# The last pass of a four-layer graph kernel: one-hot products over 128 columns, and another split between fetching and gathering

## The reference

```python
e = jnp.concatenate((x_i, x_j - x_i), axis=1)      # x_i = x[row], x_j = x[col]
h = jnp.einsum('ec,oc->eo', e, W)                  # 64 outputs
h = h * inv + (bn_beta - bn_mean * inv)            # folded batch norm
h = h * jax.nn.sigmoid(h)
x_out = jax.ops.segment_sum(h, row, num_segments=3125)
```

## Time and profile before

| | |
|---|---|
| median of the runs | 4616.29 us |
| the profiled execution's own time | 4610.87 us |
| its span | 4609.1 us |
| TensorE matmul busy | 3653.8 us (79%) |
| VectorE busy | 2905.1 us (63%) |
| GpSimd busy | 2938.6 us (64%) |
| ScalarE busy | 802.6 us (17%) |
| mean granted clock | 0.868 |

### The profile page before, as it was taken

One profiled execution on the slowest core, in us unless ns is written; L12 is line 12 of the kernel. 1 busy time (PEld: TensorE's weight loads), 2 busy tenths in 40 slices (PEclk: granted clock), 3 DMA queues, 4 the chain that ended last, 5 costly groups with the idle time before them and its releaser, 6 DMA issues. The chain is left out here.

```text
span 4609.1 us, 84700 instructions
## 1 busy us (share of the span) xinstructions
PE 3653.8 (79%) x22275; PEld 2687.5 (58%) x22286; DVE 2905.1 (63%) x10170; ACT 802.6 (17%) x2131; POOL 2938.6 (64%) x2961
## 2 busy tenths in 40 slices
PE   1279248888879999997887858888578785889999
PEld 1279125544543444443666646666466664888999
DVE  7987349999981111115888878888788886223544
ACT  0000002222220000001222213222222221100111
POOL 2677768877778888801777747777477773777200
PEclk9999969999989999998999979999799986555555
DMA  4310023334469999994222232222322222333211
GB/s 145 108 35 10 17 68 89 89 90 91 91 161 358 363 356 356 363 356 169 62 63 62 62 58 63 63 62 62 58 63 62 62 62 50 92 90 88 48 38 35
DMA packets 307333, 532.16 MB, mean 115 GB/s; under 512 B 160747, under 2 KB 206092, under 8 KB 305710
## 3 DMA queue, kind: packets, MB, share of 16 engines
q1 hardware_dynamic: 135291, 377.26, 23.5%
q0 software_dynamic: 89024, 112.37, 12.6%
q10 hardware_dynamic: 82800, 40.01, 3.0%
HBM read 469.36 MB, written 59.59 MB: 115 GB/s over the span
## 5 line engine op out<-in xcount | busy, mean ns | idle before, releaser
L967 POOL DMA_INDIRECT arena<-table,arena x1664 | 1715.9, 1031 | 851.4 <-issue 452.0
L1826 PE MATMUL ps<-arena 128*128 128x96 f32 (+6 forms) x9664 | 1571.3, 340 | 475.7 <-DVE arena L1140 153.5
L1826 PEld LDWEIGHTS ps<-arena 128*128 128x128 f32 (+6 forms) x9664 | 1167.8, 211 | 840.3 <-issue 449.4
L1826 PE MATMUL ps<-arena,nodes 125*64 125x500 f32 (+2 forms) x3144 | 653.0, 537 | 34.6 <-DMA arena<-dense 24.0
L921 POOL DMA_INDIRECT rows_src<-stage,stage_at x400 | 482.8, 1207 | 117.2 <-issue 111.2
L1826 PE MATMUL ps<-nodes,arena 125*128 (+1 forms) x2640 | 508.1, 384 | 60.4 <-DVE arena L1626 37.6
L950 POOL DMA_INDIRECT rows_dst<-stage,arena x400 | 403.0, 1008 | 227.3 <-issue 124.3
L1826 PEld LDWEIGHTS ps<-nodes,arena 125*128 125x128 f32 (+1 forms) x2640 | 495.8, 296 | 70.3 <-issue 48.5
L1393 DVE TENSOR_SCALAR arena<-iota_row_b,arena 128x128 f32<-128x128 bf16 x1664 | 458.6, 297 | 0.0
L1826 PEld LDWEIGHTS ps<-arena,nodes 125*64 125x64 f32 (+1 forms) x3144 | 246.3, 137 | 351.0 <-issue 319.3
L1493 DVE TENSOR_TENSOR nodes<-nodes,ps 125x256 f32 (+1 forms) x70 | 27.5, 393 | 610.2 <-PE ps L2034 610.2
(11 more groups left out here) (335 smaller groups left out, 4155.6 us busy)
## 6 DMA issues: line engine op xcount, KB each, us to landing
arena<-dense SPq DMA_DIRECT2D x240, 750.0 KB, 7.3
nodes<-dense SPq DMA_DIRECT2D x60, 750.0 KB, 8.0
dense<-arena ACTq DMA_DIRECT2D x150, 250.0 KB
nodes<-turn_rows SPq DMA_DIRECT2D x140, 256.0 KB, 3.2
arena<-dense SPq DMA_DIRECT2D x60, 500.0 KB, 7.5
arena<-table,arena POOLq DMA_INDIRECT x1664
arena<-rows_dst SPq DMA_DIRECT2D x208, 96.0 KB
arena<-dense SPq DMA_DIRECT2D x6, 2000.0 KB, 22.0
```

What stands on the lines that cost most here:

```text
L967: nc.gpsimd.indirect_dma_start(rows[:, u, k, 0:width], None, frm, bass.IndirectOffsetOnAxis(ap=p[:, c, j, c_other:c_other + 1].bitcast(I32 ...
L1826: return nc.tensor.matmul(to, lhsT, rhs, start=start, stop=stop, skip_group_check=True)
```

## The change

Each block of the two tables gets 64 columns of zeros behind it (`WIDE = 128`), and the pair steps and the local products stream 128 columns in place of 64; the products of `sum_up3` keep their 96. A bank then holds four tiles (`PG = 4`), and the wait for a free bank is made for each 8 steps; the loop still goes round once for 16 steps, now with two such waits in it. TensorE fetches 120 tiles and 296 are gathered; this makes 720 steps and 45 iterations. `store` has 296 places, so the last 120 tiles are gathered into places that the first 120 leave, each unit behind a wait for the sum that reads its place. The tables of one side move to the arena; the zeros of `msg3` and of the tables are written by GpSimd, and VectorE's memset of `msg3` goes.

```diff
-PT = 104
+PT = 120
-PG, PB, PB0, BURST = 8, 4, 4, 16
+PG, PB, PB0, BURST = 4, 4, 4, 8
+WIDE = 2 * D
+SLOTS = T - PT
...
+        gathered_rows = nodes[0:LO, 3:5, :].rearrange("p i (h d) -> p (i h d)", h=HI).rearrange("p (h d) -> p h d", d=WIDE)
...
-        store = carve([128, T, D])
+        local_rows = carve([LO, HI, WIDE])
+        store = carve([128, SLOTS, D])
...
         def lin3(u):
-            return ps[:, 4 + u % 2, 0:K * D].rearrange("p (k d) -> p k d", k=K)
+            return ps[:, 4 + u % 2, :].rearrange("p (k d) -> p k d", k=K)
+        def place_of(t):
+            return t if t < SLOTS else t - SLOTS
...
-            write_projected(table_sb, t1[:], LAYERS + 1)
+            write_projected(table_sb, gathered_rows[:, :, 0:D], LAYERS + 1)
...
             pool.wait_ge(turn_out, 16 * 2)
+            hold(pool, hs_ready, LAYERS + 2)
+            nc.gpsimd.memset(msg3[:, :, :, D:MW], 0.0)
+            nc.gpsimd.memset(local_rows[:, :, D:WIDE], 0.0)
+            nc.gpsimd.memset(gathered_rows[:, :, D:WIDE], 0.0)
+            pool.drain()
+            pool.sem_inc(cleared, 1)
...
                     t = PT + n * K + k
+                    if t >= SLOTS and t % K == 0:
+                        pool.wait_ge(sums_made, place_of(t) // K + 1)
                     nc.gpsimd.indirect_dma_start(
-                        store[:, t, :], None, table,
+                        store[:, place_of(t), :], None, table,
...
-                nc.vector.tensor_copy(group_of(t1, q), projected(q, D, 2 * D, 2 * D)).then_inc(proj_read, 1)
+                nc.vector.tensor_copy(group_of(gathered_rows, q), projected(q, D, 2 * D, 2 * D)).then_inc(proj_read, 1)
...
-            link(nc.vector.memset(msg3, 0.0))
...
-                nc.vector.tensor_tensor(s3[:, u % PR], store[:, u * K:(u + 1) * K, :], lin3(u), ALU.add).then_inc(sums_made, 1)
+                at_ = place_of(u * K)
+                nc.vector.tensor_tensor(s3[:, u % PR], store[:, at_:at_ + K, :], lin3(u)[:, :, 0:D], ALU.add).then_inc(sums_made, 1)
...
-                nc.scalar.copy(store[:, g * PG:(g + 1) * PG, :].rearrange("p t d -> p (t d)"), ps[:, bank, :]).then_inc(rows_kept, 1)
+                sums = ps[:, bank, :].rearrange("p (t d) -> p t d", d=WIDE)[:, :, 0:D]
+                nc.scalar.copy(store[:, g * PG:(g + 1) * PG, :], sums).then_inc(rows_kept, 1)
                 a.wait_ge(rows_kept, g + 1)
-                nc.scalar.copy(ps[:, bank, :], zeros[:]).then_inc(pair_bank_free, 1)
+                nc.scalar.copy(sums, zeros[:, 0:PG * D].rearrange("p (t d) -> p t d", d=D)).then_inc(pair_bank_free, 1)
...
-            with pe.Fori(0, PS // BURST) as i:
-                need3 = load_values(pe, pair_need[0:1, bass.ds(i, 1)], 1, PT // PG + 1)[0]
-                pe.reg_alu(at_least_one, need3, 1, ALU.max)
-                hold(pe, pair_bank_free, at_least_one)
-                for e in range(BURST // K):
-                    offs = load4(pair_off[0:1, bass.ds(i * BURST + e * K, K)], PB0 * 512, 8 * 512 - D)
-                    blks = load4(pair_blk[0:1, bass.ds(i * BURST + e * K, K)], 0, (HI - 1) * D)
-                    pe.wait_ge(turned_made, i * (BURST // K) + (e + 1))
+            pe.wait_ge(cleared, 1)
+            with pe.Fori(0, PS // (2 * BURST)) as i:
+                for e in range(2 * BURST // K):
+                    if e % (BURST // K) == 0:
+                        b = e * K // BURST
+                        need3 = load_values(pe, pair_need[0:1, bass.ds(i * 2 + b, 1)], 1, PT // PG + 1)[0]
+                        pe.reg_alu(at_least_one, need3, 1, ALU.max)
+                        hold(pe, pair_bank_free, at_least_one)
+                    offs = load4(pair_off[0:1, bass.ds(i * 2 * BURST + e * K, K)], PB0 * 512, 8 * 512 - WIDE)
+                    blks = load4(pair_blk[0:1, bass.ds(i * 2 * BURST + e * K, K)], 0, (HI - 1) * WIDE)
+                    pe.wait_ge(turned_made, i * (2 * BURST // K) + (e + 1))
                     for k in range(K):
-                        ins = mm(flat[:, bass.ds(offs[k], D)], ohT3[0:LO, e % PR, k * 128:(k + 1) * 128],
-                                 gathered_table[:, bass.ds(blks[k], D)], start=False, stop=False)
+                        ins = mm(flat[:, bass.ds(offs[k], WIDE)], ohT3[0:LO, e % PR, k * 128:(k + 1) * 128],
+                                 gathered_table[:, bass.ds(blks[k], WIDE)], start=False, stop=False)
...
                 for k in range(K):
-                    ins = mm(lin3(u)[:, k, :], ohT3[0:LO, (PE_ + u) % PR, k * 128:(k + 1) * 128], local_table[:, bass.ds(offs[k], D)], start=k == 0)
+                    ins = mm(lin3(u)[:, k, :], ohT3[0:LO, (PE_ + u) % PR, k * 128:(k + 1) * 128], local_table[:, bass.ds(offs[k], WIDE)], start=k == 0)
```

More of the change, by code:

```diff
@@ L90 @@
 PH = PC * 128 // 2
-PG, PB, PB0, BURST = 8, 4, 4, 16
+PG, PB, PB0, BURST = 4, 4, 4, 8
+WIDE = 2 * D
+SLOTS = T - PT
 PE_, PU, PR, PK = PS // K, T // K, 4, 6
-assert PT % PG == 0 and PS % BURST == 0 and PH <= TABLE_W and BURST <= (PB - 2) * PG and (PE_ + PU) % 2 == 0
+assert PT % PG == 0 and PS % (2 * BURST) == 0 and 512 == PG * WIDE and PH <= TABLE_W and BURST <= (PB - 2) * PG and (PE_ + PU) % 2 == 0
 AB, AP, MW = 7, 68, 96
@@ L404, in gnn_kernel @@
         msg3 = carve([128, PR, K, MW])
-        store = carve([128, T, D])
-        assert used[0] >= high_to
+        local_rows = carve([LO, HI, WIDE])
+        store = carve([128, SLOTS, D])
+        used[0] = max(used[0], high_to)
         pair_off = carve([1, PS], I32)
@@ L598, in gnn_kernel @@
         sums_made = sem("sums_made")
+        cleared = sem("cleared")
         silu_made = sem("silu_made")
@@ L1269, in _ @@
                 link(nc.vector.tensor_scalar(block_of, ps[0:1, bank, 0:T], -1.0, None, ALU.add))
-                link(nc.vector.tensor_scalar(tab_at[:, side, :], block_of, float(3 * D if side else D), None, ALU.mult))
+                link(nc.vector.tensor_scalar(tab_at[:, side, :], block_of, float(3 * D if side else WIDE), None, ALU.mult))
                 link(nc.vector.tensor_scalar(bank_no, block_of, 1.0 / AB, -(0.5 - 0.5 / AB), ALU.mult, ALU.add))
@@ L1313, in _ @@
                 nc.vector.tensor_scalar(tile_col[:, c:c + 1], ps[:, 4, 2 * c:2 * c + 1], iota_p[:, 0:1], float(128 * c), ALU.add, ALU.add)
-            nc.vector.tensor_scalar(blk_i.rearrange("p (b t) -> p b t", b=2), ps[0:1, 2:4, 0:PH], float(D), None, ALU.mult)
+            nc.vector.tensor_scalar(blk_i.rearrange("p (b t) -> p b t", b=2), ps[0:1, 2:4, 0:PH], float(WIDE), None, ALU.mult)
             link(nc.vector.tensor_scalar(step_code[:], ps[:, 4, 0:2 * PC].rearrange("p (c x) -> p x c", x=2)[:, 1, :], 128.0, None, ALU.mult))
@@ L1330, in _ @@
             link(nc.vector.scalar_tensor_tensor(tile_tmp, tile_tmp, -float(PB * PG), tile_row, ALU.mult, ALU.add))
-            link(nc.vector.tensor_scalar(off_i, tile_tmp, float(D), float(PB0 * 512), ALU.mult, ALU.add))
+            link(nc.vector.tensor_scalar(off_i, tile_tmp, float(WIDE), float(PB0 * 512), ALU.mult, ALU.add))
             floor_of(need_f, tile_row[:, BURST - 1:PS:BURST], PG)
@@ L1610, in _ @@
                 v.wait_ge(proj_done, groups_before(LAYERS + 1) + (q + 2))
-                nc.vector.tensor_tensor(group_of(t2, q), projected(q, 0, D, 2 * D), over_group(bnr[:, 1, :], q), ALU.add)
-                nc.vector.tensor_copy(group_of(t1, q), projected(q, D, 2 * D, 2 * D)).then_inc(proj_read, 1)
+                nc.vector.tensor_tensor(group_of(local_rows, q), projected(q, 0, D, 2 * D), over_group(bnr[:, 1, :], q), ALU.add)
+                nc.vector.tensor_copy(group_of(gathered_rows, q), projected(q, D, 2 * D, 2 * D)).then_inc(proj_read, 1)
             v.wait_ge(proj_read, groups_before(LAYERS + 2) + 1)
@@ L1814, in _ @@
                 bank = PB0 + g % PB
-                nc.scalar.copy(store[:, g * PG:(g + 1) * PG, :].rearrange("p t d -> p (t d)"), ps[:, bank, :]).then_inc(rows_kept, 1)
+                sums = ps[:, bank, :].rearrange("p (t d) -> p t d", d=WIDE)[:, :, 0:D]
+                nc.scalar.copy(store[:, g * PG:(g + 1) * PG, :], sums).then_inc(rows_kept, 1)
                 a.wait_ge(rows_kept, g + 1)
-                nc.scalar.copy(ps[:, bank, :], zeros[:]).then_inc(pair_bank_free, 1)
+                nc.scalar.copy(sums, zeros[:, 0:PG * D].rearrange("p (t d) -> p t d", d=D)).then_inc(pair_bank_free, 1)
+            a.wait_ge(cleared, 1)
             for u in range(PU):
@@ L2155, in _ @@
             ins.then_inc(pair_bank_free, PB)
-            gathered_table = nodes[0:LO, 3, :]
-            local_table = nodes[0:LO, 4, :]
-            with pe.Fori(0, PS // BURST) as i:
-                need3 = load_values(pe, pair_need[0:1, bass.ds(i, 1)], 1, PT // PG + 1)[0]
-                pe.reg_alu(at_least_one, need3, 1, ALU.max)
-                hold(pe, pair_bank_free, at_least_one)
-                for e in range(BURST // K):
-                    offs = load4(pair_off[0:1, bass.ds(i * BURST + e * K, K)], PB0 * 512, 8 * 512 - D)
```

(12 more changed lines are left out.)

## The result

| | before | after |
|---|---|---|
| median of 4 runs | 4614.14 us (4607.81 to 4619.28) | 4783.81 us (4777.17 to 4786.21) |
| span of the profiled execution | 4609.1 us | 4784.4 us |
| mean granted clock | 0.868 | 0.876 |

The ratio is 1.0366, with a 95% interval of 1.0348 to 1.0384. The forecast was 4542 us, so the time lies 242 us above it and outside the range.

A forecast was written before the change was run, and what follows sets the result against it. TensorE's line was taken as the bound in the last pass: its sequencer in the first stage, the low clock in the second. +40 - 115 + 1 = -74 us gave a 4542 us median, range 4505 to 4600.

The forecast's parts named there:

- An iteration becomes 7.94 + 0.7 = 8.65 us: Last pass, pair-step loop (first stage): the added bank wait lengthens each of 45 iterations; stage +40 us.
- the comb: First stage, TensorE: 7.10 us of matmuls per iteration, next piece 7.94 us after the one before; forecast 8.6 to 8.7.
- The second bank wait: First stage, TensorE's sequencer: another wait for a free bank per iteration costs 0.7 us, range 0.6 to 0.9.
- The first stage gains nothing from a high clock: Last pass, pair steps: TensorE's sequencer is the bound, so a faster clock is worth nothing there.
- The second stage gets 2.4 GHz from its products of 128 columns: Last pass, local products and sums: a unit takes 2.3 us in place of 3.41, 104 units, -115 us.
- The first rival: Second stage: clock stays at 1.2 GHz and the stage at 354 us; 4657 us in all, 10% chance.
- The gathers are off the path: Last pass, GpSimd: gathers done at about 4449 us, not on the path, with 75 us to spare.
- The clock was to go up early in the first stage: Pair steps of the last pass: 3.6 us of matmuls per iteration at 2.4 GHz, of no use there.
- 80%: Second stage, sign of being right: TensorE's matmuls fill about 80% of a 2.3 us unit.
- the first stage did not speed up: Rival for the pair steps: an iteration falls to 4.4 us, total 4350 us, 7% chance.
- the second bank wait was not hidden: Rival for the pair steps: the added wait is hidden, -33 us more, 4509 us, 5% chance.
- the second stage found no other limit: Rival: a wait chain or late one-hots limit that stage to 2.7 us a unit, 4584 us, 12% chance.

The follow-up runs named there:

- a_align: Kernel after, with the pair-step tables moved to start at a multiple of four words (31320 in place of 31317); 4540.96 us, ratio 0.9839.
- b_off1: Kernel before, with the same pair-step tables one word later in SBUF (33281 in place of 33280); 4854.61 us, ratio 1.0515.
- a_pair64: a_align with the pair steps streaming 64 columns again, local products keeping 128; 4534.63 us, ratio 0.9834.
- a_local64: a_align with the second stage's local products streaming 64 columns again, pair steps keeping 128; 4654.37 us, ratio 1.0082.

## Why the prediction was wrong

**The step that failed** is "An iteration becomes 7.94 + 0.7 = 8.65 us". The mechanism was right: the sequencer bounds this stage, and each operation added to it adds to the comb. The term that was mis-sized is the one that was not written as a term: the eight loads of four registers inside the 7.94 us. They were carried over from the earlier trace rows at 0.33 us, and took 1.00. That is 5.4 us in an iteration and 241 us in 45; the miss was 242. The section on the change spoke of the run-time tables only as numbers that change; that their place changed, in one line of the diff, the prediction didn't price, and it gave that instruction no bound from above. (The profiled execution took 4786.2 us where 4537 was forecast, 249 more: 243 are the comb's, 45 times 5.41, and the rest is about the late start of the stage.) `a_align` and `b_off1` show the cause from both sides, each with one number changed.

In the rows of this stage the cost could not have been read: its loads of four all took about 0.33 us. But the trace of before held it elsewhere. Between 619 and 1305 us ScalarE's sequencer loads seven registers at a time from `bin_end` (L1715, recorded at L661), 25 times, each load seven words behind the one before, so that only every fourth begins at a multiple of four words. The first nine of them, in rows of one that begins at a multiple and of the three behind it that don't (count, ns least/median/most, first and last start):

```profile
L661 ACTq TENSOR_LOAD <-arena x1: 1327/1327/1327, 619.3 to 619.3; - x1
L661 ACTq TENSOR_LOAD <-arena x3: 1610/1641/1753, 702.8 to 755.0; - x3
L661 ACTq TENSOR_LOAD <-arena x1: 1014/1014/1014, 783.3 to 783.3; - x1
L661 ACTq TENSOR_LOAD <-arena x3: 1661/1674/1841, 809.0 to 861.7; - x3
L661 ACTq TENSOR_LOAD <-arena x1: 972/972/972, 888.9 to 888.9; - x1
```

The seven that begin at a multiple take 0.97 to 1.33 us, the eighteen others 1.56 to 1.87, and the traces of `b_off1` and `a_align` show the same split. It is another engine, beside the traffic of another part of the program, so this gives the direction and not the size. The kernel's own source points there too: for other tables that are loaded four at a time it asserts the start (`assert KEEP_FROM % 4 == 0 and TABLE_W % 4 == 0 and PER_BODY % 4 == 0`), and for `pair_off` and `pair_blk` it does not. With the sequencer known as the bound, and the operand of its loads moved, that was reason enough for a range that reached higher, or a rival.

**What was right**, as `a_align` shows without the misplaced tables (4540.96 us against the 4542 forecast; that it is so close is partly chance, as its four runs spread over 5 us):

- The second bank wait adds 0.75 us to an iteration, 8.69 against 7.94, where 0.7 was forecast.
- The first stage gains nothing from a high clock: `a_pair64` takes 8.70 us an iteration at 0.50, `a_align` 8.69 at 0.75.
- The second stage gets 2.4 GHz from its products of 128 columns, 2.29 us a unit ((4524.3 - 4288.9) / 103) against 2.3. The first rival, a clock that stays at 1.2 GHz, was built as `a_local64`: 4654 us where the prediction had 4657.
- The gathers are off the path. In `a_align` the last one starts at 4451.0, 73 us before the last sum. In the kernel after, GpSimd stood 410 us at the wait for places, behind the late first stage, and its last gather still came 75 us before the last sum, as the row shows:

```profile
L1010 POOL DMA_INDIRECT arena<-table,nodes x296: 938/944/1206, 3900.1 to 4696.5; - x148
```

**What was wrong without effect on the time.** The clock was to go up early in the first stage. In the kernel after it stood at 0.50 there, and in `a_align` it went both ways. The matmuls of `a_align` in order of time show it, in groups of eight of the same kind:

```profile
4102.65 1.15 PE L1845 MATMUL ps<-nodes,arena 125*128 x8 [0.54 <-issue]
4105.58 1.16 PE L1845 MATMUL ps<-nodes,arena 125*128 x8 [1.77 <-issue]
4107.25 1.85 PE L1845 MATMUL ps<-nodes,arena 125*128 x8 [0.51 <-issue]
4109.67 3.78 PE L1845 MATMUL ps<-nodes,arena 125*128 x16 [0.57 <-DVE arena L1642]
```

1.15 us for eight is the high clock, 1.85 the low. And TensorE's matmuls fill 95% of the second stage (200.41 of 210 us), not 80%. That share doesn't make the array the limit. The weight loads of `a_align` there, in order of time, over two units:

```profile
4400.45 0.97 PEld L1845 LDWEIGHTS ps<-arena 128*128 128x128 f32 x8 [0.16 <-issue]
4401.61 2.06 PEld L1845 LDWEIGHTS ps<-arena 125*128 125x128 f32 x16 [0.19 <-issue]
4403.89 1.71 PEld L1845 LDWEIGHTS ps<-arena 125*128 125x128 f32 x13 [0.22 <-issue]
```

Within a row they start 0.11 us apart, so that the 16 of a unit want 1.8 us of its 2.29, and the engine waits for issue in between. This speaks for the sequencer, as the prediction had it; no run changed the sequencer's work in this stage to prove it. The other rivals did not come: the first stage did not speed up, the second bank wait was not hidden, and the second stage found no other limit.

**A comparison that the prediction got wrong.** It holds the price of a weight load in the Trainium skill, TensorE: Matmul & The Clock Gate (section LDWEIGHTS), against its rows. Columns over 1.2 GHz are 0.107 us for 128 columns, an estimate by that page, and the 0.11 us of the earlier trace rows at the high clock agrees with it. What doesn't fit is the 0.22 us at the low clock. No term of the sum hung on it.

**The rule on busy engines** that the prediction weighed: the Trainium skill, TensorE: Matmul & The Clock Gate (section Why this matters for your kernels), would have the engine kept busy for its full clock. `a_local64` is busy for 330 of 330 us at 0.50, and `a_align` for 96% at 1.00, with the same count of products and wider ones. The case speaks against reading the rule by the busy row.

## What to carry to other kernels

Where a sequencer's register loads from SBUF are the bound, the place of their table is a parameter of the kernel: put it at a multiple of four words, assert it, and look at it again whenever a buffer ahead of it changes size. When a change moves the operand of the instruction that sets the pace, its duration in the old trace is no longer known, even if the instruction isn't in the diff. And measure each half of a double change by itself: here the wide local products were worth 113 us and the wide pair steps nothing that could be measured, while leaving the whole first stage out of the kernel before was worth 174 us.

## What the runs showed of the hardware

Medians of TensorE's sequencer loading registers from SBUF, in the last pass of these kernels:

| registers in one load | where it begins | us |
|---|---|---|
| 1 | at any word | 0.31 |
| 2 | a multiple of 4 words, or 2 past it | 0.54 |
| 4 | a multiple of 4 words | 0.33 |
| 4 | 1 or 2 words past one | 1.00 |
| 8 | a multiple of 8 words | 0.59 |

A load of four that begins off its multiple costs about as much as three of one; what the hardware does in it the trace doesn't show. Loads of eight that begin elsewhere, and TensorE's loads of four at a start 3 words past a multiple, were not run. ScalarE's loads of seven between 619 and 1305 us take 1.0 to 1.3 us at a multiple of four words, and 1.6 to 1.9 at 1, 2 or 3 past one. The table holds for the last pass: in that earlier part of the kernel before, TensorE's loads took up to 0.75 us.
